# Decoder layer on one core: low parts of the context's pieces made by GpSimd in the first batch, the rank of batch 1 four slots later, and the last batch's router recast

## The reference

```
x = x + self_attention(layernorm(x))         # 16 heads of 64, causal, relative position bias
x = x + cross_attention(layernorm(x), ctx)   # 16 heads of 16; ctx is 4 x 1601 x 256; q and k RMS-normed
x = x + moe(layernorm(x))                    # 40 classes: 32 experts and 8 that pass x on; top 6
```

## Time and profile before

| | us |
|---|---|
| median of 3 runs | 1346.81 (1345.29 to 1347.44) |
| profiled execution, its own time | 1349.23 |
| its span | 1347.5 |
| busy: TensorE, weight loads | 1232.5, 761.1 |
| busy: VectorE, ScalarE, GpSimd | 716.3, 865.8, 695.8 |
| granted TensorE clock, mean | 0.972 |

### The profile page before, as it was taken

How to read it: one execution, slowest core, us unless ns; L and a number is a source line. 1 busy time by engine, 2 the same in 40 slices (tenths; PEclk the granted TensorE clock), 3 DMA queues, 4 the chain that set the end, 5 groups by cost and what they waited for, 6 DMA issues and landing times.

```text
span 1347.5 us, 27953 instructions
## 1 busy us (share of the span) xinstructions
PE 1232.5 (91%) x8788; PEld 761.1 (56%) x8788; DVE 716.3 (53%) x2370; ACT 865.8 (64%) x1691; POOL 695.8 (52%) x775
## 2 busy tenths in 40 slices
PE   5999999999999885899999999999989899899955
PEld 4666776776676474433333333333322589799954
DVE  6666466557555557563136313632553366566647
ACT  4666456546645425668977897789989447577730
POOL 1776557557656602355217611762377447766640
PEclk9999999999999897999999999999999889899988
DMA  7976466556535621100011001010283646665649
GB/s 238 351 253 223 166 231 229 204 175 232 184 140 193 201 63 34 33 23 12 18 40 35 9 17 40 11 35 1 94 294 123 245 141 201 223 185 177 179 152 385
DMA packets 146277, 195.08 MB, mean 145 GB/s; under 512 B 12592, under 2 KB 133056, under 8 KB 145488
## 3 DMA queue, kind: packets, MB, share of 16 engines
q1 hardware_dynamic: 135376, 162.97, 36.5%
q0 software_dynamic: 10752, 30.26, 6.3%
HBM read 71.01 MB, written 122.18 MB: 143 GB/s over the span
## 4 chain that ended last, share of the span: by engine, by line
PE 55%; ACT 16%; issue 12%; DVE 8%; DMA 3%; POOL 3%; ACTq 2%; SPq 0%; POOLq 0%; DVEq 0%
PE sa_pf L347 11%; ACT xa_probs L1387 8%; PE xa_banks L1226 7%; PE xa_banks L1241 6%; PE sa_po L422 5%; PE sa_ps L396 5%; PE xa_banks L1109 5%; PE sa_ptr L407 5%; PE sa_pf L380 4%; ACT mo_xs_t L2054 3%; DMA mo_w_all<-parts 2%; ACTq L2058 2%; PE mo_banks L2007 2%; ACT mo_silu L2076 1%; PE mo_banks L1957 1%
## 5 line engine op out<-in xcount | busy, mean ns | idle before, releaser
L1387 ACT ACTIVATE xa_probs<-xa_banks 128x1024 f32<-128x1024 f32 (+1 forms) x416 | 401.9, 1045 | 85.8 <-PE xa_banks L1226 84.9
L334 POOL TENSOR_SCALAR sa_probs<-sa_probs,sa_recip 128x128 f32<-128x128 f32 (+3 forms) x256 | 274.8, 1087 | 176.4 <-DVE sa_recip L585 176.2
L465 ACT ACTIVATE sa_probs<-sa_probs,sa_neg_max 128x128 f32<-128x128 f32 (+3 forms) x256 | 141.9, 555 | 148.0 <-DVE sa_neg_max L522 148.0
L1241 PE MATMUL xa_banks<-xa_probs,xa_v_one 128*17 128x512 f32 (+1 forms) x1664 | 219.6, 600 | 6.8 <-ACT xa_q_aug L1333 4.5
L1226 PE MATMUL xa_banks<-xa_q_aug,xa_k_aug 32*128 32x512 f32 (+1 forms) x1664 | 153.8, 443 | 13.6 <-issue 3.7
L1938 POOL DMA_INDIRECT parts<-mo_y,mo_dest x128 | 122.9, 960 | 61.8 <-issue 33.1
L2007 PE MATMUL mo_banks<-mo_xs_t,mo_gu 128*128 128x128 f32 x1024 | 138.5, 279 | 0.0
L522 DVE CUSTOM_DVE_ANT_0 sa_probs<-sa_ps,sa_toeplitz 128x128 f32<-128x128 f32 (+3 forms) x256 | 115.5, 488 | 38.7 <-PE sa_ps L396 35.9
L2007 PEld LDWEIGHTS mo_banks<-mo_xs_t,mo_gu 128*128 128x128 f32 x1024 | 128.0, 196 | 0.1
L2061 ACT ACTIVATE mo_gu<-mo_w_all 128x512 f32 x128 | 80.7, 630 | 67.6 <-issue 53.4
L1226 PEld LDWEIGHTS xa_banks<-xa_q_aug,xa_k_aug 32*128 32x128 f32 (+1 forms) x1664 | 62.0, 180 | 107.3 <-ACT xa_probs L1387 74.6
(11 more groups left out here) (309 smaller groups left out, 2310.9 us busy)
## 6 DMA issues: line engine op xcount, KB each, us to landing
rows<-sa_blank SPq DMA_DIRECT2D x128, 548.0 KB, 3.5
mo_xs<-rows SPq DMA_DIRECT2D x128, 137.0 KB
parts<-sa_blank SPq DMA_DIRECT2D x96, 128.0 KB, 3.6
mo_w_all<-parts SPq DMA_DIRECT2D x16, 768.0 KB, 14.5
xa_raw<-in_ctx_t SPq DMA_DIRECT2D x24, 256.0 KB, 2.8
mo_w_all<-in_gate_up_p SPq DMA_DIRECT2D x2, 2816.0 KB, 17.2
sa_toeplitz<-extended_bias SPq DMA_DIRECT2D x8, 512.0 KB, 7.4
mo_w_all<-in_down_p SPq DMA_DIRECT2D x2, 2048.0 KB, 15.5
```

The source lines that it names most:

```text
L334: pool.tensor_scalar(probs[:, t % SLOTS, 0:w], probs[:, t % SLOTS, 0:w], recip[:, col:col + 1], None, ALU.mult).then_inc(probs_ready, 1)
L465: act.activation(probs[:, t % SLOTS, 0:w], probs[:, t % SLOTS, 0:w], ACT.Exp, bias=neg_max[:, i:i + 1], scale=-1.0, accum_out=sums[:, i:i ...
L1241: last = pe.matmul(banks[32 * i:32 * i + XD + 1, 6 + group % 2, :], v_one[b % 2][0:m, c, 4 * g + i, :], probs[0:m, (2 * j + i // 2) % RING ...
L1387: act.activation(probs[0:m, n % RING, :, :], banks[0:m, 2 * (n % 3):2 * (n % 3) + 2, :], ACT.Exp).then_inc(probs_ready, 1)
```

## The change

Five things are changed.

In cross attention: `low_part`, on GpSimd, takes the place of VectorE's subtraction for pieces 2 to 6 of batch 0, at the same slots. ("rk", 1, 0) moves from slot 15 to slot 19 of batch 3. The last group's output is added to x by VectorE, right after it has made it; GpSimd skips it.

In the last batch's router: TensorE transposes x itself and classifies that; VectorE subtracts mean times the sum of the classifier's rows (`class_mean`, from an early matmul) and multiplies with the reciprocal root after the maximum is taken off. Normalised rows are made piece by piece in waits. What depends on the first three batches' counts alone (tiles of the early part, their ends and steps) is made by GpSimd in `early_tiles`, 24 chained steps, after its 72 sends and the last add of x; the prefix sum over all four batches is one scan. TensorE's count adds the mask's four parts in PSUM. `steer_ready` is set by the copy of `steer`. The filler is cut: 24, 20, 26, 12 become 3 and 2, 20, 8, 16. ScalarE does one Silu after the exponential, ahead of the loop.

SyncE loads `acc` in three parts, at tiles 56, 72 and 88.

```diff
@@ ROUTE
-             (B - 1, 10): ("rl", 1, 0), (B - 1, 15): ("rk", 1, 0), (B - 1, 22): ("rx", 2, 0),
+             (B - 1, 10): ("rl", 1, 0), (B - 1, 19): ("rk", 1, 0), (B - 1, 22): ("rx", 2, 0),
@@ cross_attention, run_gpsimd
+            def low_part(g):
+                n = cut_size(g)
+                pool.wait_ge(ct0_hi_done, g + 1)
+                pool.tensor_tensor(ct_lo[g % 2][:, :, 0:n], raw[g % 2][:, :, 0:n],
+                                   ct_hi[g % 2][:, :, 0:n].bitcast(F32), ALU.subtract
+                                   ).then_inc(ct_ready, 1)
...
+                        if g == QUADS * B - 1:
+                            continue
...
                     if nb == 0:
+                        if s in CUT_AT:
+                            low_part(CUT_AT[s])
                         continue
@@ cross_attention, run_vector, evacuate and low_first
+                    if group == QUADS * B - 1:
+                        wait_out(dve, f)
+                        cols = x_sb[:, :, (QUADS - 1) * 4 * XD:]
+                        dve.tensor_tensor(cols, cols, o_norm[:].rearrange("p t j d -> p t (j d)"), ALU.add
+                                          ).then_inc(x2_part, 1)
...
-                if s in CUT_AT:
-                    g = CUT_AT[s]
-                    n = cut_size(g)
-                    dve.wait_ge(ct0_hi_done, g + 1)
-                    dve.tensor_tensor(ct_lo[g % 2][:, :, 0:n], raw[g % 2][:, :, 0:n],
-                                      ct_hi[g % 2][:, :, 0:n].bitcast(F32), ALU.subtract
-                                      ).then_inc(ct_ready, 1)
@@ experts, run_sync
+    TOKENS_AT = {56: 0, 72: 1, 88: 2}
...
                 if t == EARLY:
                     sp.wait_ge(sent[1], 16 * TT * TOP_K)
-                    sp.dma_start(acc[:], x2.rearrange("b (t p) d -> p (b t) d", p=P)[:, 0:TT * LAST, :]
+                if t in TOKENS_AT:
+                    b = TOKENS_AT[t]
+                    sp.dma_start(acc[:, TT * b:TT * (b + 1), :], x2[b].rearrange("(t p) d -> p t d", p=P)
                                  ).then_inc(acc_in, 16)
@@ experts, early_tiles (new), run_gpsimd
+            pool.wait_ge(early_out, 1)
+            chain.then_wait(pool.tensor_scalar(counts[:], counts[:], 0.5 - 0.5 * P, TO_TILES, ALU.add, ALU.add))
+            chain.then_wait(pool.tensor_scalar(filled_n, counts[:], TO_TILES, 1.0 / P, ALU.subtract, ALU.mult))
+            held = early_n[2]
+            for i in range(5):
+                at = ZEROS - 2 ** i
+                chain.then_wait(pool.tensor_tensor(early_n[i % 2][:, ZEROS:], held[:, ZEROS:],
+                                                   held[:, at:at + E_ROUTED], ALU.add))
+                held = early_n[i % 2]
...
         def run_gpsimd(pool):
+            kept.through(pool)
+            kept.stored(pool)
+            assert early_tiles(pool) == EARLY_STEPS
             pool.wait_ge(row_ready, 1)
@@ experts, run_tensor
-            keep_busy(24)
-            pe.wait_ge(xn_ready, 1)
+            kept.sent_ready(pe)
+            pe.matmul(banks[:, 2, 0:E_ROUTED], ones_r[:], picked[:, 0:E_ROUTED], start=True, stop=True
+                      ).then_inc(early_psum, 1)
...
+            keep_busy(3)
+            kept.through(pe)
             for c in range(KD):
                 for t in range(TT):
-                    last = pe.transpose(banks[:, c, t * P:(t + 1) * P], packed[:, t, c * P:(c + 1) * P], ident[:])
+                    last = pe.transpose(banks[:, c, t * P:(t + 1) * P], own_x[:, t, c * P:(c + 1) * P], ident[:])
                 last.then_inc(xt_psum, 1)
-            pe.wait_ge(kept.router_in, 32)
+            keep_busy(2)
             pe.wait_ge(xt_out, KD)
...
             last.then_inc(lg_psum, 1)
             keep_busy(20)
+            pe.wait_ge(early_ready, 2)
             pe.wait_ge(mask_ready, 1)
@@ experts, run_scalar
+            act.wait_ge(early_psum, 1)
+            act.activation(counts[:], banks[:, 2, 0:E_ROUTED], ACT.Copy).then_inc(early_out, 1)
...
+            act.wait_ge(const_ready, 2)
+            act.activation(silu[0][:, 0:1], ident[:, 0:1], ACT.Silu)
@@ experts, run_vector (the new chain from the logits and from the count)
+            chain.then_wait(dve.tensor_tensor(scores[:], logits, class_mean[:], ALU.subtract))
+            chain.then_wait(dve.tensor_reduce(row_max[:], scores[:], AX.X, ALU.max))
...
+            normalise(0)
             dve.wait_ge(kept.router_in, 32)
+            dve.wait_ge(early_ready, 2)
             dve.wait_ge(exp_ready, 1)
...
+            chain.then_wait(dve.tensor_scalar(ends[:], banks[:, 7, 0:E_ROUTED], 0.5 * P - 0.5, TO_TILES,
+                                              ALU.add, ALU.add))
+            chain.then_wait(dve.tensor_scalar(n_tiles, ends[:], TO_TILES, 1.0 / P, ALU.subtract, ALU.mult))
+            all_tiles = all_n[0][:, ZEROS:]
+            chain.then_wait(dve.tensor_tensor_scan(all_tiles, ones[:, 0:E_ROUTED], n_tiles, 0.0, ALU.mult, ALU.add))
+            dve.wait_ge(early_ready, EARLY_STEPS)
+            dve.scalar_tensor_tensor(out=steps[:], in0=n_tiles, scalar=late_rows[:], in1=early_steps[:],
+                                     op0=ALU.mult, op1=ALU.add)
...
+            normalise(1)
...
+            dve.tensor_copy(steer[:], banks[0:1, 5, 0:2 * N_TILES]).then_inc(steer_ready, 1)
+            chain.then_wait(dve.tensor_scalar(row_no[:], banks[:, 5, 0:N_TILES], tile_no[:], None, ALU.add))
+            normalise(2)
+            normalise(3)
```

More of the change, by code:

```diff
@@ L2232, in run_vector @@
                                                 op0=ALU.mult, op1=ALU.add)
[L2233 to L2235 removed]
+            chain.then_wait(last)
+            dve.wait_ge(acc_in, 16 * LAST)
             for t in SUM_ORDER:
```

207 lines of the change are left out of this document (114 added, 93 removed).

## The result

The changed kernel takes **1335.51 us** (median of 4 runs, 1333.84 to 1336.63); the kernel before took 1347.12 beside it (4 runs, 1345.29 to 1348.94). The ratio is 0.9913 [0.9894, 0.9932]. The profiled execution took 1333.84 us with a span of 1332.1, so in the pair of profiled executions the gain is 15.4 us, where the sum said 20.9.

A forecast was written before the change was run, and what follows sets the result against it. TensorE was taken as busy nearly throughout attention, with one serial chain between the stages. Terms −1.0 −3.0 −10.8 −6.1 = −20.9 us from the median 1346.81 gave a forecast of 1326 us, range 1320 to 1334.5.

The forecast's parts named there:

- the base: Starting time: the median of runs, 1346.81, 2.4 lower than the profiled execution, giving 1325.9 instead of 1328.3.
- C: Between cross attention and the first expert tile: shorter router chain and earlier weights, −10.8 us (ends −11.5 and −8).
- A: Batch 0 of cross attention: low parts moved from VectorE to GpSimd, −1.0 us (ends −3.4 and +1.5).
- the hits: Batch 0 of cross attention: VectorE operations delayed beside GpSimd work, 0.45 us each, one or two of them taken.
- Rival 2: Batch 0 of cross attention: moving low parts costs +1.5 us, TensorE meeting pieces 2 and 6 later; 1328.4, chance 0.10.
- B: Batch 3 of cross attention: ranking batch 1 at slot 19 removes the slot 15 stall, −3.0 us (ends −3.9 and 0).
- two sends more in flight make it 1076.2: Before the expert loop: GpSimd sends in flight move the weights' landing from 1075.8 to 1076.2.
- t: End of the last output add of cross attention, forecast at 1058.4, from which the router chain's steps are counted.
- rival 1: Between the stages: GpSimd's chain is the bound, loop 2.5 us later, 1328.5; chance 0.15.
- DMA falls quiet at 1079.2 ... They land at 1075.8: Before the expert loop: DMA fell quiet 17.4 us after the weights' issue, so weights issued at 1058.4 land at 1075.8.
- D: Expert loop: token rows in three loads remove the stall at tile 40, −6.1 us (ends −6.7 and −4).
- The ring: Expert loop: the ring of 16 results loses a us of slack; not priced, at most +1.

The follow-up runs named there:

- c_alone: Changed kernel with low parts, ranking slot and token loads as before, so only the stretch between the stages stays changed: 1339.55 us, ratio 0.9932.
- set 3: Set without breaks: the changed kernel again and three variants of it, sharing runs of the kernel before, which took 1349.83 us.
- fine_undo_b: Changed kernel with twelve token loads and the ranking of batch 1 back at slot 15: 1456.47 us, ratio 0.9915.
- less_down: Changed kernel without the last load of expert weights (2,048 KB), other numbers written there: 1459.33 us, ratio 0.9892.
- hold_tiles: Changed kernel in which the first tile load waits for the weights' last byte: 1462.12 us, ratio 0.9885.
- fine_mix: Changed kernel with twelve token loads and low parts of pieces 2 and 3 back on VectorE: 1453.4 us, ratio 0.9892.
- after_again: The changed kernel itself, run once more in another set: 1461.27 us, ratio 0.9896.

## Why the prediction was wrong

The direction and the order of the parts were right; all four terms of the sum were too large, and the base was moved the wrong way. The step with the largest error is the landing of the weights in C: they are used 22.0 us after their issue where I had 18.6. The prediction named "weights land later than 18 us after their issue" as a sign that it is wrong; they landed after 21.0, and after 18.5 already in the trace that it was read from.

**A, forecast −1.0, measured −0.4.** The steps held up to the hits: piece 2 came 0.6 later as worked out. I took "one or two" hits of 0.45. In the profiled run there were three, of 0.43, 1.0 and 0.86 us (0.63, 1.22 and 1.28 where 0.20, 0.20 and 0.42 are usual), 2.3 of the 3.4 us taken off VectorE. TensorE's wait before the last piece, which I expected to fall from 2.83 us, is 2.98. The number of hits was near, the price was not: the earlier trace rows show one hit on one short operation, and it is no bound, since an operation can be held for nearly all of GpSimd's 1.28 us. Which operations were stretched also has an order: two of TENSOR_SCALAR and one TENSOR_TENSOR with both inputs in SBUF, while the TENSOR_REDUCE of 1.22 us ahead of them, half beside GpSimd's work, kept its time. The Trainium skill (SBUF — State Buffer, Who interferes with whom) says just this: the first two kinds can be blocked fully by a GpSimd operation issued before them, a TENSOR_REDUCE can't on this chip. The trace agrees: all three stretched operations started after GpSimd's and ended within 0.3 us of its end. The TENSOR_REDUCE started before GpSimd's, and neither of the two was held. The rule's A of about zero is nearer to the measured 0.4 than my −1.0, and says in advance which work to look at. Rival 2, A costing 1.5, is refuted.

**B, forecast −3.0, measured −2.0 to −2.4 on the path to the last add.** The mechanism was right: from the end of GpSimd's add of the 12th head group's output to the end of the last add it takes 98.4 us before, 98.0 in c_alone, which has the new last add too, and 95.7 to 96.1 with B; the short wait stands at slot 23 (0.93, forecast 0.7). What failed is a step in C, "two sends more in flight make it 1076.2", 0.4 us: with B and the earlier add the sends cost the weights 1.0 to 1.6 us more than in c_alone. A and B together brought 1.6 us in set 3 for 4.0 in the sum. That sends in flight are the cause rests on four traces with B against one without, and on the 20.5 to 20.7 us in the sets where the sends were through. The first load's landing, 2.1 to 2.3 us later with sends in flight than in c_alone, says the same. Both runs that were to settle it (fine_undo_b and its repeat) fell in broken sets, so it is likely and not shown by an experiment that moves the sends alone.

**C, forecast −10.8, measured −10.3** in the total of c_alone, −9.6 in its trace up to the gate of tile 36. The chain went almost as worked out: layernorm to logits, mask at t + 9.6 (forecast 9.2), steering numbers at t + 14.9 (13.7), GpSimd's 22 steps at 0.34 us (0.31) ended at 1068.53, before VectorE's operation at 1068.91 that needs them, so rival 1 did not occur. I had named the weights as the end of the stretch, which less_down confirms. But "DMA falls quiet at 1079.2 ... They land at 1075.8", with ScalarE's copy at 1077, took a quiet window for the landing. From issue to use are 22.0 us, not 18.6. Of these 3.4, some 1.1 is the misreading: in the trace of before the weights land 18.5 us after their issue, not 17.4. Another 1.1 goes with the packet that comes late behind the instruction packet, which no run isolates: in the 13 traces of changed kernels in which the sends were through, the weights land after 19.6 to 19.8 us. The sends cost 1.4 (21.05 us in the changed kernel) where I had 0.4, and the load of a number ahead of the copy 0.9 where I had 0.8. The Trainium skill (DMA: Bandwidth & Descriptors, Anatomy of one DMA — SWDGE (gpsimd) path) puts most of a DMA's fixed cost of some 2 us between its last byte and its semaphore, for GpSimd's path; this load comes from SyncE, and 0.4 us lie there (hold_tiles), so the page's figure doesn't explain the gap. Between copy and gate the loop was faster than I had it (3.8 us for 4.2), and the first four gates gave back 1.5 (3.85 us instead of 5.32) where I had 0.4, so the first gate is 2.9 late and the fourth 1.9. Those 1.5 are no lasting gain: from the first gate to that of tile 36 it takes 56.2 to 57.0 us in all five traces of changed kernels without breaks, and 56.8 before.

**D, forecast −6.1, measured −3.9** by totals, −5.4 by the trace in the same set. The stall in the trace of before was 6.9 us where two other traces have 5.6 and 5.8; I took one sample for the size. The three loads cost 0.4 to 1.2 us in all where I had 0.6.

**The ring, "at most +1"**: 0.9 between tiles 3 and 36 in the pair of traces, 0.8 to 1.2 in the other three with A and B, 0.1 in c_alone; no run tells whether the ring is the cause. **The end**: 1.1 us in the loads of the parts, not foreseen. After the last gate 49.7 to 49.8 us follow in the five traces of changed kernels without breaks, 48.7 in the one of the kernel before; no run tested it, and it stays open.

**The base.** I took the gain from the median of three runs, 1346.81, 2.4 under the profiled execution. The kernel before scatters by 8 us and its median in other sets without breaks was 1347.12 and 1349.83; the changed kernel's runs lie within 3. My 1326 was so 2.3 lower than the same sum from the profiled execution, 1328.3. Of the miss of 9.5, 5.5 are the terms above (1333.84 against 1328.3 by the profiled executions): along the table 2.0 up to the gate of tile 3 (14.8 forecast, 12.8 measured), 2.4 in the loop (6.1 and 3.7) and 1.1 at the end. Of the rest, 2.3 are this base, and 1.7 is what the profiled execution of the changed kernel lies under its median. The range, down to 1320 but only up to 1334.5, had the good ends of all terms in it, but not all poor ones, although these have something in common: each term was read from one trace.

No version beats the changed kernel with an interval that shows it; the twelve token loads with the low parts of pieces 2 and 3 on VectorE (fine_mix) are the one to run again: 0.6 us better in the trace at the first place and perhaps up to 2 at the second. They have run only in broken sets, where the total shows nothing.

## What to carry to other kernels

Where DMA seems to fall quiet is not where its load has landed: the last of sixteen engines decides, and a mean over a wide window hides it. Read the landing from the view of the load's line, and how soon it is used from an engine that really waits for it. When a chain is cut short, list what is still in flight when it now ends, since a queue that used to be done by then becomes part of the next stretch's load. And work handed to an engine that shares a way to memory should go where that engine's result isn't needed at once: three of five pieces moved won more than all five.

## What the runs showed of the hardware

From the end of the last packet of 6,656 KB of weights to the last update of their semaphore lay 0.4 us (hold_tiles), and 0.93 us more passed before ScalarE's first copy, which loads a number first. A packet on the instruction queue seems to hold up one packet of the weights: in 18 traces one started when the other ended and took 1.08 us instead of 0.61. In the 13 of them with no sends in flight it was the weights' last, and the load landed 1.1 to 1.3 us later after its issue than in the kernel before. Two loads issued 15 us after each other end together when the first is large: the first tile's rows landed 4.6 to 6.7 us after their issue behind the weights, 2.1 and 2.3 without them in flight (less_down, hold_tiles).

The same kernel took 1334 us in one set and 1461 in another. In the long ones ScalarE's exponentials were no slower (1.02 us each, after 980 us in both traces), but TensorE's matmuls were, since its granted clock was lower (a mean of 0.946 against 0.977; `times_v` took 0.71 us and not 0.60). Much of the time went in breaks, in which these engines stood still while GpSimd went on sending, as here in after_again, ScalarE and TensorE:

```profile
991.79 1.02 ACT L1398 ACTIVATE xa_probs<-xa_banks 128x1024 f32<-128x1024 f32 x1 [13.08 <-remote]
...
992.87 1.23 PE L1237 MATMUL xa_banks<-xa_q_aug,xa_k_aug 32*128 32x512 f32 x8 [13.30 <-issue]
```

The trace names no engine as the cause ("remote", "issue"), and no run here tells what it is. The sets ran on different chips (three with breaks, one without), so a cause outside the kernel is as open as one in it. I had not expected that a kernel's time can differ by a tenth in this way while the ratio of two kernels stays (0.9896 and 0.9888).
